# Feed-forward of layer 0: stores of x without waits on each other, issued later, behind the fetch of raw weights; sums for ternary weights two steps ahead

## The chip, the cores and the metric

One NeuronCore of a Trainium2 chip runs the whole program. The metric is the device time of one execution in microseconds; the median of several is given. TensorE (PE) does the matmuls, VectorE (DVE), ScalarE (ACT) and GpSimd (POOL) the elementwise work, and SyncE (SP) issues every DMA.

## What is computed

Two transformer layers over x, 4 x 1024 tokens of width 512 (4096 rows), 16 heads. Layer 0 ends with the feed-forward at issue here, layer 1 uses ternary weights that have to be made from the given float weights:

```python
# layer 0, end
x = x + out @ Wout
h2 = layer_norm(x, ln2_g, ln2_b)
x = x + (gelu(h2 @ W1 + b1) @ W2 + b2)          # W1: 512 x 2048, W2: 2048 x 512

# layer 1: every weight of ada1, ada2, qkv, proj, fc1, fc2
def weight_quant(w):
    s = 1.0 / clip(mean(abs(w)), EPS)            # one mean for the whole matrix
    return clip(round(w * s), -1, 1) / s
def adaln(x, c, g, w, b):
    scale, shift = split(bitlinear(c, w, b))     # the products with ada1 and ada2
    return rmsnorm(x, g) * (1 + scale) + shift
```

## The kernel before, in words

The program is a row of stages; each ends in a barrier of all engines. The change is in `stage_fc0`, which runs from about 1545 to 2315 us of the execution. It computes the feed-forward in 8 blocks of 512 rows (i = 0 to 7), and in each block over 16 chunks of 128 hidden units (f). Together that is 128 steps, u = 16 i + f, and every engine has its own loop over u. All order between engines is by semaphores that are written out by hand.

In a step TensorE does `fc1(u)`, 12 matmuls into `pf` (name `mhi`, `mlo`, `w1h`, `w1l` for the two halves of float32 operands), and `fc2(u - 2)`, 12 matmuls into the four accumulators `pacc`. ScalarE makes `w1h`, the gelu `gf` and its high half `gh`. VectorE makes, in this order, `w1l` for step u + 2, `gl` of step u (after ScalarE's `gh`), at f = 1 of the next block the four additions `xM<-pacc,xM` (the new x of the block; semaphore `s_x2`), at f = 2 to 5 one addition `xb<-xM,bpb` each (`with_bias`: x plus the bias of the next projection, into the single buffer `xb2`, so it waits until the store of the previous one has landed), and last one item of side work, `vector_work(*work[u])`.

The side work turns layer 1's weights into ternary ones while the feed-forward runs. The list `work` has for each matrix, in the order ada1, ada2, qkv, proj, fc1, fc2, one `sum` item per piece of 128 x 1024 numbers, then `mean`, then one `tern` item per piece, and for the two ada matrices an `emb` item. A `sum` reduces a piece to `asum`; TensorE adds the partial sums over the partitions (`tensor_work`, into `pmisc`), one step later than the item; `mean` makes the scale on VectorE out of that product; a `tern` item is three VectorE operations on the piece. The matrices have 4, 4, 6, 2, 8 and 8 pieces, so `work` has 72 items before. `tern` of an ada matrix also has a product on TensorE (`pmisc<-tern,cqT`), which waits for it in the step behind.

SyncE's loop `sync_program` issues in step u: the stores of the finished block (`store_x2`, 4 DMAs `s_x<-xM` of 256 KB) at f = 0, one `store_x2b` (`s_x2b<-xb`, 256 KB) at f = 2 to 5, then `sync_work(*work[u + 1])`, which fetches the raw piece for the next item (`wraw`, 512 KB, two buffers, so it waits until VectorE is through with the piece two before), `sync_store(*work[u - 1])`, the store of a ternary piece (256 KB), and the loads of the next block. SyncE is in order: while it waits for one semaphore, nothing behind is issued.

Of the kernel before, what the change touches and what calls it, by code (L numbers as in the profile page):

```python
# [14 lines left out]
NBLK, TPB = T // BLK, BLK // P  # L15
NT = T // P
# [884 lines left out]
def pieces(n):  # L901
    rows, cols = SHAPE[n]
    wide = CH if cols % CH == 0 else D
    tall = CH // wide
    return [(slice(c * P, (c + tall) * P), slice(n0, n0 + wide), wide)
            for c in range(0, rows // P, tall) for n0 in range(0, cols, wide)]


def stage_mlp0(K):

    nc, a, pe, dve, act, pool, sp = K.nc, K.a, K.pe, K.dve, K.act, K.pool, K.sp
    outer = ExitStack()
    with outer:
        sb = lambda name, shape, dt=F32: outer.enter_context(nc.sbuf_tensor(name, shape, dt))
        w1, w2 = sb("w1", [P, DC, F]), sb("w2", [P, FC, D])
        hf = [sb(f"hf{i}", [P, DC, BLK]) for i in range(2)]
        s_hf, s_w = [K.new_sem() for _ in range(2)], K.new_sem()
        stage_outproj(K, w1, w2, hf, s_hf, s_w)
        stage_fc0(K, w1, w2, hf, s_hf, s_w)


def load_h2(K, hf, s_hf, i):

    K.nc.sync.dma_start(hf[i % 2][:], K.h2_s[:, i * BLK:(i + 1) * BLK].rearrange("(c p) t -> p c t", p=P)).then_inc(*s_hf[i % 2].up(16))
# [201 lines left out]
def stage_fc0(K, w1, w2, hf, s_hf, s_w):  # L1126
    nc, a, pe, dve, act, pool, sp = K.nc, K.a, K.pe, K.dve, K.act, K.pool, K.sp
    LAG = 2
    with Stage(K, "M") as S:
# [10 lines left out]
        gl = [S.sb(f"gl{i}", [P, BLK], F32R) for i in range(3)]  # L1140
        bpb, xb2 = S.sb("bpb", [P, D]), S.sb("xb2", [P, D])
        s_bpb, s_xb, s_xbst = S.sem(), S.sem(), S.sem()
        x_l = S.loads("xM", 4, [P, D])
        tern = S.stores("tern", 2, [P, 2 * D], BF16)
        pf_r = S.ps_ring("pf", 3, [P, BLK])
# [5 lines left out]
        half_rows = [slice(32 * half, 32 * half + B) for half in range(2)]  # L1151
        cqT = S.sb("cqT", [P, DC, B], BF16)
        s_b1, s_cond, s_em, s_emst = S.sem(), S.sem(), S.sem(), S.sem()
        s_f1, s_gf, s_gh, s_gl, s_f2, s_x2, s_xst = (S.sem() for _ in range(7))
        s_asum, s_tot, s_totr, s_tern, s_raw, s_cn, s_cT, s_cq, s_ada, s_emb, s_embr = (S.sem() for _ in range(11))
        work = []
        for i, n in TERN_ORDER:
            work += [("sum", i, n, c, piece) for c, piece in enumerate(pieces(n))]
            work.append(("mean", i, n, 0, None))
            work += [("tern", i, n, c, piece) for c, piece in enumerate(pieces(n))]  # L1160
            if n.startswith("ada"):
                work.append(("emb", i, n, 0, None))
# [11 lines left out]
        def sync_work(kind, i, n, c, piece):  # L1174
            if kind == "emb":
                j = i - 4
                sp.wait_ge(s_emb, 2 * j + 2)
                for half, r in enumerate(half_rows):
                    nc.sync.dma_start(K.emb_s[j + 1][:, half, :], cn2[r, :]).then_inc(*s_emst.up(16))
                if j == 0:  # L1180
                    sp.wait_ge(s_emst, 32)
                    load_ada_bias("L1_cond_b_ada2")
                return
            if kind == "mean":
                return
            rows, cols, wide = piece
            buf, s = raw.take(sp, (kind, n, c), 1, (s_raw, at[kind, n, c] + 1))
            nc.sync.dma_start(buf[:].rearrange("p (c n) -> p c n", n=wide), a[SRC[n]][rows, cols].rearrange("(c p) n -> p c n", p=P)).then_inc(*s.up(16))

        def load_ada_bias(name):  # L1190
            for half, r in enumerate(half_rows):
                nc.sync.dma_start(cn2[r, :], a[name][half * D:(half + 1) * D].partition_broadcast(B)).then_inc(*s_em.up(16))

        def sync_store(kind, i, n, c, piece):
            if kind != "tern" or n.startswith("ada"):
                return
            rows, cols, wide = piece
            k = at["store", n, c]
            buf, s = tern.of(k)
            sp.wait_ge(s_tern, k + 1)  # L1200
            nc.sync.dma_start(K.tern_s[n][rows, cols].rearrange("(c p) n -> p c n", p=P),
                              buf[:].rearrange("p (c n) -> p c n", n=wide)).then_inc(*s.up(16))

        def sync_program():
            nc.sync.dma_start(b1T[:], a["L0_cond_b1_cols"]).then_inc(*s_b1.up(16))
            nc.sync.dma_start(bpb[:], a["L1_cond_b_proj"].partition_broadcast(P)).then_inc(*s_bpb.up(16))
            for r in half_rows:
                nc.sync.dma_start(cn2[r, :], a["cond_1024"]).then_inc(*s_cond.up(16))
            sync_work(*work[0])
            nc.sync.dma_start(b2b[:], a["L0_cond_b2"].partition_broadcast(P)).then_inc(*s_b2.up(16))  # L1210
            for u in range(N_STEP):
                i, f = divmod(u, FC)
                if u == 1:
                    sp.wait_ge(s_cT, 1)
                    load_ada_bias("L1_cond_b_ada1")
                if f == 0 and i > 0:
                    store_x2(i - 1)
                if i > 0 and 0 <= f - 2 < TPB:
                    store_x2b(i - 1, f - 2)
                if u + 1 < len(work):  # L1220
                    sync_work(*work[u + 1])
                if 1 <= u <= len(work):
                    sync_store(*work[u - 1])
                if f == 1 and i + 1 < NBLK:
                    if i >= 1:
                        sp.wait_ge(s_hl, DC * i)
                    load_h2(K, hf, s_hf, i + 1)
                if f == 8:
                    for t in range(TPB):
                        rows = rows_of(i, t)  # L1230
                        x, s = x_l.take(sp, (i, t), 1, (s_xst, 16 * (TPB * i + t + 1)), (s_xb, TPB * i + t + 1))
                        nc.sync.dma_start(x[:], K.x1_s[rows, :]).then_inc(*s.up(16))
            store_x2(NBLK - 1)
            for t in range(TPB):
                store_x2b(NBLK - 1, t)
            sp.wait_ge(s_xst, 16 * NT)
            sp.wait_ge(s_xbst, 16 * NT)
            sp.wait_ge(s_emst, 64)
            tern.done(sp)

        def rows_of(i, t):
            return slice(i * BLK + t * P, i * BLK + (t + 1) * P)

        def store_x2(i):
            for t in range(TPB):
                sp.wait_ge(s_x2, TPB * i + t + 1)
                if TPB * i + t:
                    sp.wait_ge(s_xst, 16 * (TPB * i + t))
                nc.sync.dma_start(K.x2_s[rows_of(i, t), :], x_l.at[i, t][0][:]).then_inc(*s_xst.up(16))

        def store_x2b(i, t):
            sp.wait_ge(s_xb, TPB * i + t + 1)
            nc.sync.dma_start(K.x2b_s[rows_of(i, t), :], xb2[:]).then_inc(*s_xbst.up(16))
# [22 lines left out]
                op.then_inc(*s_f2.up())  # L1276

        def tensor_work(kind, i, n, c, piece):
            if kind == "mean":
                q = [m for _, m in TERN_ORDER].index(n)  # L1280
                pe.wait_ge(s_asum, sum(len(pieces(m)) for _, m in TERN_ORDER[:q + 1]))
                if q >= 2:
                    pe.wait_ge(s_totr, q)
                    pe.wait_ge(s_embr, 4)
                elif q == 1:
                    pe.wait_ge(s_embr, 2)
                else:
                    pe.wait_ge(s_cq, 1)
                nc.tensor.matmul(misc[:, 0:len(pieces(n))], K.ones[:], asum[:, 0:len(pieces(n))], start=True, stop=True).then_inc(*s_tot.up())
            if kind == "tern" and n.startswith("ada"):  # L1290
                k = at["store", n, c]
                pe.wait_ge(s_tern, k + 1)
                pe.wait_ge(s_totr, i - 3)
                for half in range(2):
                    op = nc.tensor.matmul(misc[32 * half:32 * half + B, :], cqT[:, c, :], tern.of(k)[0][:, half * D:(half + 1) * D],
                                          start=c == 0, stop=c == DC - 1)
                op.then_inc(*s_ada.up())
# [75 lines left out]
                nc.scalar.activation(gh[u % 3][:], gf[u % 2][:], ACT.Copy).then_inc(*s_gh.up())  # L1373

        def vector_work(kind, i, n, c, piece):
            q = [m for _, m in TERN_ORDER].index(n)
            if kind == "sum":
                buf = raw.ready(dve, (kind, n, c))
# [59 lines left out]
        def vector_program():  # L1438
# [41 lines left out]
            for t in range(TPB):  # L1480
                with_bias(NBLK - 1, t)

        sync_program()
        tensor_program()
        scalar_program()
# [748 lines left out]
```

## Time and profile before

| what | value |
|---|---|
| median of 3 runs | 3868.43 us (3863.33 to 3868.81) |
| the profiled execution, its own time | 3865.6 us |
| its span in the trace | 3863.7 us |
| mean granted TensorE clock | 0.968 |
| TensorE busy over the whole span | 93% |
| VectorE, ScalarE, GpSimd busy | 69%, 60%, 50% |

The profile gives each instruction's start and length in microseconds from the span's start, and for a wait the instruction that ended it. The profiled execution took 1.9 us more than its span, and 2.8 us less than the median of the runs.

### The profile page before, as it was taken

What the parts mean: (1) busy time and instruction counts of PE and PEld (TensorE: products, weight loads), DVE (VectorE), ACT (ScalarE), POOL (GpSimd) and SP (SyncE); (2) the same over time, 40 slices, a digit from 0 to 9 for tenths busy, and PEclk for the clock granted to TensorE, in tenths of its full rate; (3) what the DMA queues carried; (4) which work ended last, traced back from release to release, by engine and by line L of the source; (5) the groups of instructions that cost most, each with busy time, mean ns of one, the idle gap of its engine ahead of it and who ended that gap; (6) DMA issues with size and microseconds to landing.
All of it is one profiled execution on the core that took longest, in us unless ns stands there. A gap on an engine that the chain in (4) does not pass through costs nothing. (4 is left out here: it accounts for less than half of the span.)

```text
span 3863.7 us, 68702 instructions
## 1 busy us (share of the span) xinstructions
PE 3588.0 (93%) x25924; PEld 2519.3 (65%) x25924; DVE 2666.8 (69%) x4271; ACT 2306.9 (60%) x4011; POOL 1921.6 (50%) x2187
## 2 busy tenths in 40 slices
PE   8997999999999989899999986889999999995999
PEld 7885777767777767777778863446666666652555
DVE  4335888888888866667753327867777777755987
ACT  2225888888888855333333326745555555554988
POOL 1003555555555533444444436646666666663554
PEclk9998999999999999999999998979999999997999
DMA  5546333333323139334431116853334333314221
GB/s 187 186 162 164 64 70 64 70 64 69 62 59 64 40 131 338 104 107 155 148 104 44 50 55 234 313 106 73 64 76 81 66 70 79 74 32 137 83 77 50
DMA packets 284776, 403.16 MB, mean 104 GB/s; under 512 B 89704, under 2 KB 146540, under 8 KB 283930
## 3 DMA queue, kind: packets, MB, share of 16 engines
q1 hardware_dynamic: 284448, 398.78, 37.3%
q8 instruction: 207, 3.39, 0.4%
q14 instruction: 121, 0.99, 0.1%
HBM read 248.95 MB, written 148.93 MB: 103 GB/s over the span
## 5 line engine op out<-in xcount | busy, mean ns | idle before, releaser
L634 POOL TENSOR_SCALAR biastile<-dist,ascale 128x1024 f32<-128x1024 f32 x512 | 574.9, 1123 | 489.4 <-DVE mn L588 476.2
L796 ACT ACTIVATE PT<-st 128x512 f32<-128x512 f32 x1024 | 544.9, 606 | 419.1 <-PE st L730 415.3
L810 DVE TENSOR_REDUCE mn<-s 128x1 f32<-128x1024 f32 x512 | 596.4, 1216 | 273.7 <-PE s L720 273.7
L873 POOL TENSOR_TENSOR two<-PT 128x1024 f32<-128x1024 f32 x256 | 603.5, 2377 | 305.0 <-ACT PT L796 304.9
L588 DVE CUSTOM_DVE_ANT_0 Sn<-sp,biastile 128x1024 f32<-128x1024 f32 x512 | 621.9, 1215 | 78.5 <-PE pt L521 46.7
L559 ACT ACTIVATE Sn<-Sn,mn 128x1024 f32<-128x1024 f32 x512 | 586.9, 1146 | 18.9 <-DVE mn L588 18.8
L521 PEld LDWEIGHTS pt<-ident,Sn 128*128 128x128 f32 x4096 | 454.9, 141 | 177.5 <-issue 150.9
L521 PE MATMUL pt<-ident,Sn 128*128 128x128 f32 x4096 | 546.9, 277 | 22.1 <-DVE og L601 22.1
L549 ACT ACTIVATE PT<-pt 128x512 f32<-128x512 f32 x576 | 337.6, 598 | 136.3 <-PE pt L521 126.3
L730 PE MATMUL st<-QS,KS 98*128 98x512 f32 x1024 | 376.4, 425 | 1.3 <-ACT PT L796 1.2
L720 PE MATMUL s<-KS,QS 96*128 96x512 f32 x1024 | 353.7, 428 | 25.3 <-DMA KS<-s_khi 23.6
L1369 ACT ACTIVATE gf<-pf,b1T 128x512 f32<-128x512 f32 x128 | 88.3, 690 | 480.8 <-PE pf L1263 480.8
L551 DVE COPY PT<-pt 128x512 f32<-128x512 f32 x448 | 309.6, 691 | 87.9 <-PE pt L521 81.3
L489 PE MATMUL sp<-KS,QS 97*128 97x512 f32 x1024 | 304.7, 418 | 23.5 <-DMA KS<-cpad 18.9
L1339 POOL TENSOR_SCALAR w2h<-w 128x512 fp32r<-128x512 f32 x128 | 94.1, 735 | 414.0 <-PE pacc L1275 408.0
L510 PE MATMUL po<-PT,Vp 128*32 128x256 f32 x4096 | 273.7, 384 | 27.5 <-ACT ov L572 27.5
L730 PEld LDWEIGHTS st<-QS,KS 98*128 98x128 f32 x1024 | 192.7, 188 | 146.2 <-ACT PT L796 64.9
L1468 DVE TENSOR_TENSOR gl<-gf,gh 128x512 fp32r<-128x512 f32 x128 | 112.8, 881 | 226.4 <-ACT gh L1373 225.9
L741 PE MATMUL po<-PT,Vp 128*32 128x256 f32 x4096 | 247.3, 382 | 0.0
L720 PEld LDWEIGHTS s<-KS,QS 96*128 96x128 f32 x1024 | 176.9, 193 | 99.3 <-DVE mn L810 52.0
L489 PEld LDWEIGHTS sp<-KS,QS 97*128 97x128 f32 x1024 | 174.2, 191 | 50.3 <-issue 19.3
L1275 PE MATMUL pacc<-w2h,gh 128*128 128x512 f32 x512 | 199.6, 390 | 1.1 <-DVE xM L1475 1.1
(257 smaller groups left out, 6503.2 us busy)
## 6 DMA issues: line engine op xcount, KB each, us to landing
QS<-s_qhi SPq DMA_DIRECT2D x128, 256.0 KB, 5.1
KS<-s_khi SPq DMA_DIRECT2D x128, 256.0 KB, 6.9
KS<-s_klo SPq DMA_DIRECT2D x64, 256.0 KB, 6.2
QS<-s_qlo SPq DMA_DIRECT2D x64, 256.0 KB, 6.8
Vp<-s_v SPq DMA_DIRECT2D x64, 256.0 KB, 7.7
s_o<-og SPq DMA_DIRECT2D x32, 512.0 KB, 4.0
xA<-in_x SPq DMA_DIRECT2D x8, 1024.0 KB, 5.9
s_qhi<-qstage SPq DMA_DIRECT2D x32, 256.0 KB, 2.0
```

The costliest lines, as they stand in the source:

```text
L489: op = nc.tensor.matmul(ps[:, g * BLK:(g + 1) * BLK], qs[0:rows_s, j, t * P:(t + 1) * P], ks[0:rows_s, j, g * BLK:(g + 1) * BLK], start=Tr ...
L521: op = nc.tensor.transpose(ps[:, i, :], sn[:, (g * HALF + i) * P:(g * HALF + i + 1) * P], K.ident[:])
L549: nc.scalar.activation(dst, src, ACT.Copy).then_inc(*s_cp_act.up())
L551: nc.vector.tensor_copy(dst, src).then_inc(*s_cp_dve.up())
L559: nc.scalar.activation(sn[:], sn[:], ACT.Exp, scale=-1.0, bias=mn[n % 3][:, t:t + 1], accum_out=sums[n % 5][:, t:t + 1]).then_inc(*s_exp.up())
L588: nc.vector.tensor_tensor_reduce(sn[:], sp_r.at[s][:], bt[s % 2][:], 1.0, 3.4e38, ALU.add, ALU.min, m).then_inc(*s_min.up())
L634: nc.gpsimd.tensor_scalar(bt[s % 2][:], dist[:, t, :], K.ascale[:, n % H:n % H + 1], 1.0, ALU.mult, ALU.mult).then_inc(*s_bias.up())
L720: op = nc.tensor.matmul(ps[:, g * BLK:(g + 1) * BLK], qs[0:ROWS, j, t * P:(t + 1) * P], ks[0:ROWS, j, g * BLK:(g + 1) * BLK], start=True, ...
L730: nc.tensor.matmul(ps[:], ks_l.at[p][0][0:ROWS + 2, j, kb * P:(kb + 1) * P], qs_l.at[p][0][0:ROWS + 2, j, g * BLK:(g + 1) * BLK], start=Tr ...
L796: nc.scalar.activation(pT[n % 2][:, kb, g * BLK:(g + 1) * BLK], pst_r.at["st", u, g][:], ACT.Exp, scale=-1.0).then_inc(*s_exp.up())
L810: nc.vector.tensor_reduce(mn[n % 2][:, t:t + 1], ps_r.at[u][:], AX.X, ALU.min).then_inc(*s_min.up())
L873: nc.gpsimd.tensor_tensor(two[m % 6][:], pT[n % 2][:, 2 * k, :], pT[n % 2][:, 2 * k + 1, :], ALU.add).then_inc(*s_two.up())
```

## The change

The four stores of a block get a semaphore each, `s_xst[t]`, in place of one for all, and no longer wait for each other's landing. `store_x2` is issued at f = 2 in place of 0 and `store_x2b` at f = 3 to 6 in place of 2 to 5, and both now stand behind `sync_work` and `sync_store` of the step in place of ahead of them. Between the last `sum` and the `mean` of each matrix the list `work` gets two more items, `total` (TensorE's product over the partitions is tied to it) and `rest` (nothing). `work` has 84 items in place of 72, and every item behind the first matrix's sums moves back by 2 steps per matrix.

```diff
+        s_xst = [S.sem() for _ in range(TPB)]
...
-            work.append(("mean", i, n, 0, None))
+            work += [("total", i, n, 0, None), ("rest", i, n, 0, None), ("mean", i, n, 0, None)]
...
-                if f == 0 and i > 0:
-                    store_x2(i - 1)
-                if i > 0 and 0 <= f - 2 < TPB:
-                    store_x2b(i - 1, f - 2)
                 if u + 1 < len(work):
                     sync_work(*work[u + 1])
                 if 1 <= u <= len(work):
                     sync_store(*work[u - 1])
+                if f == 2 and i > 0:
+                    store_x2(i - 1)
+                if i > 0 and 0 <= f - 3 < TPB:
+                    store_x2b(i - 1, f - 3)
...
                 sp.wait_ge(s_x2, TPB * i + t + 1)
-                if TPB * i + t:
-                    sp.wait_ge(s_xst, 16 * (TPB * i + t))
-                nc.sync.dma_start(K.x2_s[rows_of(i, t), :], x_l.at[i, t][0][:]).then_inc(*s_xst.up(16))
+                nc.sync.dma_start(K.x2_s[rows_of(i, t), :], x_l.at[i, t][0][:]).then_inc(*s_xst[t].up(16))
...
         def tensor_work(kind, i, n, c, piece):
-            if kind == "mean":
+            if kind == "total":
```

The places where it meets the path are the changes of block. On SyncE, the one from block 2 to block 3 (steps 48 to 52) reads so before; s34 is `s_x2`, s35 the landing of the previous store, s43 the raw buffer set free, s42 a ternary piece made, s17 `s_xb`:

```order
L1249 DMA s_x<-xM 128x512 [waits s34]
L1249 DMA s_x<-xM 128x512 [waits s35,s34] x3
L1188 DMA wraw<-in_w_fc1T 128x1024 [waits s43]
L1201 DMA s_tfc<-tern 128x1024 [waits s42]
L1188 DMA wraw<-in_w_fc1T 128x1024 [waits s43]
L1201 DMA s_tfc<-tern 128x1024 [waits s42]
L924 DMA hf<-s_h 128x4x512 [waits s9]
L1253 DMA s_x2b<-xb 128x512 [waits s17]
L1188 DMA wraw<-in_w_fc1T 128x1024 [waits s43]
L1201 DMA s_tfc<-tern 128x1024 [waits s42]
```

The four stores stand ahead of the raw fetch, three of them wait for a landing too. After the change SyncE has at the change from block 1 to block 2 (steps 33 to 37), the one that falls into a run of ternary pieces; s46 is the raw buffer, s45 the ternary piece, s38 `s_x2`, s17 `s_xb`:

```order
L924 DMA hf<-s_h 128x4x512 [waits s9]
L1189 DMA wraw<-in_w_qkvT 128x2x512 [waits s46]
L1202 DMA s_tqkv<-tern 128x2x512 [waits s45]
L1249 DMA s_x<-xM 128x512 [waits s38] x4
L1189 DMA wraw<-in_w_qkvT 128x2x512 [waits s46]
L1202 DMA s_tqkv<-tern 128x2x512 [waits s45]
L1253 DMA s_x2b<-xb 128x512 [waits s17]
L1189 DMA wraw<-in_w_qkvT 128x2x512 [waits s46]
L1202 DMA s_tqkv<-tern 128x2x512 [waits s45]
L1253 DMA s_x2b<-xb 128x512 [waits s17]
```

Now the raw fetch goes first, and each `s_x2b` store stands behind a fetch and a ternary store. On VectorE at that same change of block (steps 33 to 35 after the change), s18 is the landing of the previous `s_x2b` store, s38 is `s_x2`:

```order
L1477 TENSOR_TENSOR xM<-pacc,xM 128x512 [waits s37,s15] x4
L1398 TENSOR_SCALAR wraw<-wraw,wsc 128x1024 [waits s6]
L1400 TENSOR_SCALAR wraw<-wraw 128x1024 [waits s2]
L1408 TENSOR_SCALAR tern<-wraw 128x1024 [waits s2]
L1410 ISA [waits s45]
L1334 TENSOR_TENSOR w1l<-w,w1h 128x512 [waits s33,s10]
L1470 TENSOR_TENSOR gl<-gf,gh 128x512 [waits s35]
L1438 TENSOR_TENSOR xb<-xM,bpb 128x512 [waits s18,s38]
L1398 TENSOR_SCALAR wraw<-wraw,wsc 128x1024 [waits s7]
L1400 TENSOR_SCALAR wraw<-wraw 128x1024 [waits s2]
L1408 TENSOR_SCALAR tern<-wraw 128x1024 [waits s2]
L1410 ISA [waits s45]
```

Here a ternary piece follows the four additions and each `xb`; before, this change of block had two `sum` pieces and a `mean` in these steps. The ternary pieces that fall on a change of block are those of ada2 (from step 19), qkv (33 to 37) and fc2 (80 to 83) now, and were those of ada2, fc1 and fc2 before.

## Rows read from the trace of the kernel before

**Rows 1.** The page, busy microseconds of each engine over the span
```profile
PE 3588.0 (93%) x25924; PEld 2519.3 (65%) x25924; DVE 2666.8 (69%) x4271; ACT 2306.9 (60%) x4011; POOL 1921.6 (50%) x2187
```

**Rows 2.** Timeline of TensorE: start, length; first matmuls of `fc1` in some steps
```profile
1651.41 1.20 PE L1263 MATMUL pf<-mhi,w1h 128*128 128x512 f32 x4
...
1657.38 1.20 PE L1263 MATMUL pf<-mhi,w1h 128*128 128x512 f32 x4
...
1679.60 1.20 PE L1263 MATMUL pf<-mhi,w1h 128*128 128x512 f32 x4
...
1756.84 1.07 PE L1263 MATMUL pf<-mhi,w1h 128*128 128x512 f32 x4
...
1787.46 1.07 PE L1263 MATMUL pf<-mhi,w1h 128*128 128x512 f32 x4
...
1858.44 1.07 PE L1263 MATMUL pf<-mhi,w1h 128*128 128x512 f32 x4
...
1868.96 2.07 PE L1263 MATMUL pf<-mhi,w1h 128*128 128x512 f32 x4 [4.92 <-DVE w1l L1334]
...
1877.04 1.07 PE L1263 MATMUL pf<-mhi,w1h 128*128 128x512 f32 x4
...
1882.48 1.07 PE L1263 MATMUL pf<-mhi,w1h 128*128 128x512 f32 x4
...
1953.46 1.07 PE L1263 MATMUL pf<-mhi,w1h 128*128 128x512 f32 x4
...
1972.34 1.07 PE L1263 MATMUL pf<-mhi,w1h 128*128 128x512 f32 x4
```

**Rows 3.** Timeline of VectorE, changes of block 2 to 3 and 4 to 5
```profile
1853.59 2.48 DVE L1475 TENSOR_TENSOR xM<-pacc,xM 128x512 f32<-128x512 f32 x4
1865.66 0.98 DVE L1396 TENSOR_SCALAR wraw<-wraw,wsc 128x1024 f32<-128x1024 f32 x1 [9.60 <-DMA wraw<-in_w_fc1T]
...
1868.21 0.69 DVE L1334 TENSOR_TENSOR w1l<-w,w1h 128x512 fp32r<-128x512 f32 x1
...
2042.60 2.48 DVE L1475 TENSOR_TENSOR xM<-pacc,xM 128x512 f32<-128x512 f32 x4
```

**Rows 4.** Timeline of SyncE's DMA queue, change of block 2 to 3
```profile
1854.30 6.49 SPq L1249 DMA_DIRECT2D s_x<-xM  x4
1860.84 0.42 SPq L1188 DMA_DIRECT2D wraw<-in_w_fc1T  x1
```

**Rows 5.** 10 us: busy PE, PEld, DVE, ACT, POOL; granted clock, DMA share, GB/s
```profile
1860.00:1870.00 10.00, 5.08 (x21) 3.85 (x20) 4.16 (x6) 1.84 (x3) 2.56 (x3) 0.88 0.84 282
```

**Rows 6.** Groups by line, 1540 to 2320: busy us, mean ns; idle before
```profile
L1381 DVE TENSOR_REDUCE asum<-wraw 128x1 f32<-128x1024 f32 x32 | 38.7, 1211 | 19.1 <-DMA wraw<-in_w_projT 9.4 <-DMA wraw<-in_w_ada2T 7.1 <-DMA wraw<-in_w_qkvT 2.0
L1396 DVE TENSOR_SCALAR wraw<-wraw,wsc 128x1024 f32<-128x1024 f32 x32 | 30.4, 951 | 29.4 <-DMA wraw<-in_w_fc1T 10.5 <-DMA wraw<-in_w_fc2T 10.0 <-DMA wraw<-in_w_ada2T 8.9
...
L1398 DVE TENSOR_SCALAR wraw<-wraw 128x1024 f32<-128x1024 f32 x32 | 26.1, 816 | 1.1
...
L1388 DVE TENSOR_REDUCE wmean<-pmisc 128x1 f32<-128x4 f32 (+3 forms) x6 | 1.0, 163 | 32.2 <-PE pmisc L1289 32.2
```

**Rows 7.** The tile `wraw`: duration ns min/median/max, first and last start
```profile
L1396 DVE TENSOR_SCALAR wraw<-wraw,wsc x32: 740/748/1778, 1591.7 to 1990.0; 128x1024 f32<-128x1024 f32 x32
```

**Rows 8.** DMA issues: KB each, median us to landing; 1733:1751, 1861:1863, then 1880:1888
```profile
s_tqkv<-tern SPq DMA_DIRECT2D x4, 256.0 KB, 4.3
...
hf<-s_h SPq DMA_DIRECT2D x1, 1024.0 KB, 8.0
...
s_x2b<-xb SPq DMA_DIRECT2D x2, 256.0 KB, 2.1
s_tfc<-tern SPq DMA_DIRECT2D x2, 256.0 KB, 5.2
```

**Rows 9.** The stage's end: VectorE's second `xb`, and SyncE's last stores
```profile
2306.65 0.69 DVE L1436 TENSOR_TENSOR xb<-xM,bpb 128x512 f32<-128x512 f32 x1 [6.35 <-DMA s_x2b<-xb]
...
2297.69 6.50 SPq L1249 DMA_DIRECT2D s_x<-xM  x4
```

More of the change, by code:

```diff
@@ L1153, in stage_fc0 @@
         s_b1, s_cond, s_em, s_emst = S.sem(), S.sem(), S.sem(), S.sem()
-        s_f1, s_gf, s_gh, s_gl, s_f2, s_x2, s_xst = (S.sem() for _ in range(7))
+        s_f1, s_gf, s_gh, s_gl, s_f2, s_x2 = (S.sem() for _ in range(6))
         s_asum, s_tot, s_totr, s_tern, s_raw, s_cn, s_cT, s_cq, s_ada, s_emb, s_embr = (S.sem() for _ in range(11))
@@ L1183, in sync_work @@
                 return
-            if kind == "mean":
+            if kind in ("total", "rest", "mean"):
                 return
@@ L1230, in sync_program @@
                         rows = rows_of(i, t)
-                        x, s = x_l.take(sp, (i, t), 1, (s_xst, 16 * (TPB * i + t + 1)), (s_xb, TPB * i + t + 1))
+                        x, s = x_l.take(sp, (i, t), 1, (s_xst[t], 16 * (i + 1)), (s_xb, TPB * i + t + 1))
                         nc.sync.dma_start(x[:], K.x1_s[rows, :]).then_inc(*s.up(16))
@@ L1235, in sync_program @@
                 store_x2b(NBLK - 1, t)
-            sp.wait_ge(s_xst, 16 * NT)
+            for sem in s_xst:
+                sp.wait_ge(sem, 16 * NBLK)
             sp.wait_ge(s_xbst, 16 * NT)
@@ L1278, in tensor_work @@
         def tensor_work(kind, i, n, c, piece):
-            if kind == "mean":
+            if kind == "total":
                 q = [m for _, m in TERN_ORDER].index(n)
@@ L1375, in vector_work @@
         def vector_work(kind, i, n, c, piece):
+            if kind in ("total", "rest"):
+                return
             q = [m for _, m in TERN_ORDER].index(n)
```

## The prediction

> **What bounds the kernel now.** I read the page first: TensorE is busy 93% of the span [rows 1], so a change that adds no matmul can win only where TensorE stands or runs slow. The change is confined to one stage, so next comes TensorE's timeline there, one row for the start of `fc1` in each step. The reader is to see the distance between starts: 5.44 us in a step that nothing disturbs (1877.04 to 1882.48 in [rows 2]). At four places it is longer, always about three steps behind a change of block:
>
> - i = 1: steps 18 and 19 take 1679.60 - 1657.38 = 22.2 us. Steps with an ada product run at about 5.97 here (1651.41 to 1657.38), so the loss is 22.2 - 11.9 = 10.3 us.
> - i = 2: steps 34 to 37 take 30.6 us for 4 x 5.44 = 21.8: loss 8.9.
> - i = 3: steps 51 and 52 take 1877.04 - 1858.44 = 18.6 for 10.9: loss 7.7.
> - i = 4: steps 67 and 68 take 18.9 for 10.9: loss 8.0.
>
> The sum is 34.9 us [rows 2]. In i = 3 the wait itself is 4.92 us and ended by `w1l`; the other 2.8 us are matmuls behind it at the lower clock (the four behind the wait take 2.07 in place of 1.07 us, and the 10 us around it show a mean granted clock of 0.88) [rows 2, 5].
>
> The cause is read backwards at i = 3. Step 49 starts two steps before 1858.44, at 1847.56. VectorE finishes its four additions at 1856.1 and then stands 9.60 us for a raw piece [rows 3]. SyncE issued that piece's fetch only at 1860.84, because the four stores ahead of it took from 1854.30 on, three waiting for a landing [rows 4]. So the ternary piece ends late, `w1l` for step 52 starts at 1868.21 and is done at 1868.9, 5.0 us after step 52 was due (1863.9). This gives the rule for the rest: VectorE may end the work of step u, plus 0.7 us of `w1l`, as late as three steps (16.3 us) after TensorE began step u; beyond that TensorE stands.
>
> **The change, part by part.** I count time from TensorE's start of the step with the additions (step 16 i + 1), called 0.
>
> *Stores out of the way of the fetch.* The fetch for step 16 i + 1 is now issued before SyncE waits for the additions, and VectorE finds it landed. This removes the whole chain above at all four places: -34.9 us, if nothing takes its place. Fetches at f = 2 to 5 also no longer wait for `xb`.
>
> *What takes its place.* `store_x2b(t)` now stands behind the fetch of its step, and this waits until VectorE is through with the previous step's item. Its landing sets the single buffer `xb2` free, and `xb` of the next step waits for that, ahead of that step's item. That is a loop: item ends, fetch, (ternary store), `x2b` store lands, `xb`, item. Issued ahead of a fetch the store lands in 2.1 us; stores issued right behind one need 4.3 to 5.2 [rows 8]. The 1 MB load `hf` behind four such DMAs needed 8.0, while 282 GB/s moved [rows 8, 5]. So I take a queue in which what stands ahead is moved first, at 0.28 MB/us, and a landing 1.2 us behind the last byte (2.1 less 0.9 for 256 KB). Behind a fetch alone the store lands 4.8 us after the item's end (0.45 for SyncE's issue and 4.3); behind a fetch and a ternary store another 256 KB is ahead, 5.7. Upper bounds, from the 5.2: 5.7 and 6.6. Lower bound, if loads and stores do not hold each other up: 2.1 and a little. I take 4.8 and 5.7, for the rows lie there.
>
> A ternary piece costs VectorE 0.95 + 0.82 and, for the third operation, of the same shape and taken as the second, 0.82, together 2.6, a sum 1.2, 1.3 with its hand-over [rows 6]; `xb`, `w1l`, `gl` 0.6 to 0.7 each (`xb` is 0.69 long [rows 9]). Undisturbed, the four additions start 5.0 after the step (2042.60; step 81 starts 12 steps behind 1972.34) and take 2.5 [rows 2, 3].
>
> - i = 2, now in a run of ternary pieces: item 33 ends at 7.5 + 2.6 = 10.1, item 34 at 10.1 + 1.9 + 2.6 = 14.6. From 10.1 the queue has a fetch, a ternary store and the four `x2` stores, 1.8 MB, until 16.7, then fetch, store and `x2b`, 3.7 us: landed at 21.6. Item 35 ends at 24.8, item 36 at 24.8 + 5.7 + 0.6 + 2.6 = 33.7, item 37 at 42.6. `w1l` for step 39 is done at 34.4, due at 32.6: 1.8 us; for step 40 at 43.3, due at 38.1 + 1.8: 3.4. With 2.6 of low clock behind it, as measured at i = 3, the loss is 7.8, nearly the 8.9 of now. Bounds: 0, and 10.5 with the slower landings (item 37 at 45.3).
> - i = 1: the ternary pieces stand at steps 19 to 22, without stores, and `xb` for t = 0 falls on the mean. Item 19 ends at 19.1, 20 at 27.1, 21 at 35.1; TensorE wants item 21 for its product at 33.7 (22nd step's start 28.2, one 5.44 step of matmuls). Loss 1.4, which I take without a fall of the clock. Bounds 0, and 3.2 with the slower landings and 2.6 of clock, 5.8.
> - i = 3 and 4 now have sums: items end at 8.8, 12.0, 20.3, 27.0 and at most 33.7, and `w1l` is done 3.7 us before it is due. No loss; the slower landings take 2.7 of the 3.7.
> - i = 5 is a new place with raw pieces, since the list is 12 items longer: 81 ends at 10.1, 82 at 14.6, 83 at about 23, due at 26.5. No loss.
>
> *Sums two steps ahead.* The mean's six waits for TensorE's product, 32.2 us, go [rows 6]. They are VectorE's idle time inside the 16.3 us of room, and the steps around them show no loss beyond the product itself. Gain 0. The moves it makes are counted above. The 12 more items cost nothing: 84 is less than 128.
>
> *End of the stage.* Block 7's four stores took SyncE from 2297.69 to 2304.2, and only then came the first `x2b` store, for which `xb` stood 6.35 us [rows 9]. The fourth addition ends at 2299.7, so this store can now be issued at about 2300.4 and the chain of four that ends the stage begins 3.8 us earlier; with 0.2 us for the fuller queue, -3.6. Bounds: -2.6 (a further 256 KB in the queue) and -3.8. Nothing hides it: the barrier follows.
>
> **Sum.** -34.9 + 7.8 + 1.4 - 3.6 = -29.3. The profiled execution took 3865.6, so 3836.3; it stood 2.8 below the median of the runs, so the median to expect is 3839.
>
> **A page against the trace.** In the Trainium skill, "DMA: Bandwidth & Descriptors", section "Queues, rings and completion order", each DMA engine takes the descriptors of one ring in order; this is the rule that speaks against the change, and the rows on landings agree with it. The same page ("Anatomy of one DMA") fits a DMA's time as 2.0 us plus bytes over 436 GB/s. The trace differs: 282 GB/s in a full stretch. By the page, an estimate, fetch, ternary store and `x2b` together land in 4.4 us in place of 5.7, item 37 would end at 37.1, and i = 2 would lose nothing.
>
> **Rivals.**
> - *No new wait* (22%): the `x2b` store passes the fetch, or the queue is fast enough. For it: alone it lands in 2.1 us. Against: 4.3 to 5.2 behind a fetch. Then -34.9 - 3.6: 3827 by the profile, 3830 for the median.
> - *VectorE itself is too slow at the change of block* (12%). The longest of its ternary operations took 1.78 us, against a median of 0.75 [rows 7]; GpSimd was at work beside it. If pieces 33 to 37 took 5.1 in place of 2.6 us each, i = 2 would lose 12.5 more, and the three at i = 1 7.5 + 2.6 more: gain 6.7, 3862. Against: the mean is 0.95 with such operations in it.
> - *Slower* (5%): the `xb` loop becomes the clock of all changes of block. At i = 3 and 4 it costs TensorE the 8 us that it loses now when each landing takes about 9 us; each further us costs 3 at i = 2, 3, 4 and 2 at i = 1, 11 in all. At 10 us: i = 3 and 4 13 each, i = 2 22, i = 1 14, together 62 against 34.9, less 3.6: +23, 3892. Against: 8.0 us is the longest landing seen here, with 2.5 MB in the queue.
> - *In between* (9%): a second piece of waiting at i = 1 or 5 that I have not seen, gain 8 to 18: 3850 to 3860. That the fetch would still stand behind the stores is excluded by the order of SyncE's rows.
>
> My forecast has the other 52%, 3832 to 3846 (the bounds of i = 1 and i = 2). The range, 3826 to 3853, adds "no new wait" and the near part of "in between". Differences under 0.2% (7.7 us) can hardly be told from none by this measurement; faster than that 0.90, within 0.05, slower 0.05.
>
> **What the new profile would show.** VectorE's waits for `wraw` behind the additions gone; SyncE's waits for landings of `s_x<-xM` gone; `wmean`'s wait near 0; a longer wait of `xb` for `s_x2b<-xb`, its landings at 4 to 6 us in steps 35 to 37; steps 51, 52, 67, 68 at 5.44; a loss of 5 to 10 us around step 40; TensorE's last matmul of the stage 26 us earlier, the barrier 29. I am wrong if the steps behind i = 3 or 4 are still long, or if `w1l` is late at step 40 for another cause than `xb`.

## The result, and the profile after

The changed kernel takes 3837.68 us (median of 4 runs, 3829.55 to 3840.03), the kernel before 3866.47 beside it. The ratio is 0.992, 95% interval 0.9907 to 0.9933. The forecast was 3839. The profiled execution took 3840.03 against 3865.6, 25.6 us less; its span is 3838.0.

TensorE's timeline, the starts of `fc1` at the changes of block from 1 to 2 and 2 to 3, answers to [rows 2] (in all fences: start, length; in brackets the idle time ahead and what ended it). The same source line can stand one or two lines lower than before.

```profile
1771.20 1.07 PE L1263 MATMUL pf<-mhi,w1h 128*128 128x512 f32 x4
...
1778.50 1.19 PE L1263 MATMUL pf<-mhi,w1h 128*128 128x512 f32 x4 [1.70 <-DVE w1l L1334]
...
1789.56 2.08 PE L1263 MATMUL pf<-mhi,w1h 128*128 128x512 f32 x4 [5.32 <-DVE w1l L1334]
...
1796.71 1.07 PE L1263 MATMUL pf<-mhi,w1h 128*128 128x512 f32 x4
...
1862.25 1.07 PE L1263 MATMUL pf<-mhi,w1h 128*128 128x512 f32 x4
...
1867.69 1.07 PE L1263 MATMUL pf<-mhi,w1h 128*128 128x512 f32 x4
...
1873.13 1.07 PE L1263 MATMUL pf<-mhi,w1h 128*128 128x512 f32 x4
```

Behind i = 3 the starts are 5.44 us apart, and so they are behind i = 4: the stalls of step 52 and 68 are gone. Behind i = 2 there is a new pair of waits, 1.70 and 5.32 us at steps 39 and 40. With the slow matmuls behind the second (2.08 in place of 1.07 us) the three steps from 1771.20 take 25.5 us for 16.3: a loss of 9.2, where 8.9 was lost before. The clock granted in the four us from 1789 on was 0.50, its lower level (1.2 GHz); here the columns are the length, the busy time of PE, PEld, DVE, ACT and POOL, the granted clock, the DMA share and GB/s:

```profile
1789.00:1793.00 4.00, 3.44 (x8) 2.78 (x9) 3.82 (x7) 0.00 (x0) 0.00 (x0) 0.50 0.73 224
```

At i = 1 TensorE waits 2.97 us for a ternary piece, the steps 21 to 23 take 21.2 us for 17.9, and 3.3 us are lost:

```profile
1688.34 0.38 PE L1295 MATMUL pmisc<-tern,cqT 128*4 128x512 bf16 x2 [2.97 <-DVE tern L1408]
```

VectorE in those steps answers to [rows 3]; 1744.0 is the start of step 33, five steps ahead of 1771.20:

```profile
1748.98 2.47 DVE L1477 TENSOR_TENSOR xM<-pacc,xM 128x512 f32<-128x512 f32 x4
1751.37 0.87 DVE L1398 TENSOR_SCALAR wraw<-wraw,wsc 128x1024 f32<-128x1024 f32 x1
...
1764.86 0.69 DVE L1438 TENSOR_TENSOR xb<-xM,bpb 128x512 f32<-128x512 f32 x1 [4.29 <-DMA s_x2b<-xb]
1765.47 0.75 DVE L1398 TENSOR_SCALAR wraw<-wraw,wsc 128x1024 f32<-128x1024 f32 x1
1766.25 0.98 DVE L1400 TENSOR_SCALAR wraw<-wraw 128x1024 f32<-128x1024 f32 x1
1767.27 1.66 DVE L1408 TENSOR_SCALAR tern<-wraw 128x1024 bf16<-128x1024 f32 x1
...
1774.62 0.69 DVE L1438 TENSOR_TENSOR xb<-xM,bpb 128x512 f32<-128x512 f32 x1 [4.28 <-DMA s_x2b<-xb]
...
1784.88 0.69 DVE L1438 TENSOR_TENSOR xb<-xM,bpb 128x512 f32<-128x512 f32 x1 [4.74 <-DMA s_x2b<-xb]
1785.49 1.75 DVE L1398 TENSOR_SCALAR wraw<-wraw,wsc 128x1024 f32<-128x1024 f32 x1
```

The ternary piece now follows the additions at once (it stood 9.60 us at i = 3 before), and the waiting has moved to `xb`, three times over 4 us. SyncE's queue shows why; answers to [rows 4]:

```profile
1759.24 0.38 SPq L1189 DMA_DIRECT2D wraw<-in_w_qkvT  x1
1759.67 0.47 SPq L1202 DMA_DIRECT2D s_tqkv<-tern  x1
1760.18 0.47 SPq L1253 DMA_DIRECT2D s_x2b<-xb  x1
...
1769.01 0.37 SPq L1189 DMA_DIRECT2D wraw<-in_w_qkvT  x1
1769.43 0.47 SPq L1202 DMA_DIRECT2D s_tqkv<-tern  x1
1769.94 0.47 SPq L1253 DMA_DIRECT2D s_x2b<-xb  x1
```

Item 34 ends at 1759.15, the store goes out third at 1760.18 and the addition that waits for it starts at 1764.86: 5.7 us from the item's end. Item 35 ends at 1768.93, and the same three go out again: the loop. The stores' landings, in the windows 1769:1772 and 1777:1780 (KB each, median us to landing):

```profile
s_x2b<-xb SPq DMA_DIRECT2D x1, 256.0 KB, 4.6
...
s_x2b<-xb SPq DMA_DIRECT2D x1, 256.0 KB, 6.3
```

against 2.1 ahead of a fetch [rows 8]. The groups by line (1530 to 2320) have the sums of it, and answer to [rows 6]:

```profile
L1383 DVE TENSOR_REDUCE asum<-wraw 128x1 f32<-128x1024 f32 x32 | 38.7, 1210 | 6.4 <-DMA wraw<-in_w_qkvT 3.8 <-DMA wraw<-in_w_ada2T 2.6
L1398 DVE TENSOR_SCALAR wraw<-wraw,wsc 128x1024 f32<-128x1024 f32 x32 | 34.8, 1088 | 0.0
...
L1438 DVE TENSOR_TENSOR xb<-xM,bpb 128x512 f32<-128x512 f32 x32 | 23.1, 722 | 44.0 <-DMA s_x2b<-xb 44.0
```

VectorE's waits for raw pieces went from 19.1 + 29.4 us to 6.4. Its waits for the `x2b` store rose to 44.0, from 23.1 before (same window, kernel before):

```profile
L1436 DVE TENSOR_TENSOR xb<-xM,bpb 128x512 f32<-128x512 f32 x32 | 26.0, 814 | 23.1 <-DMA s_x2b<-xb 23.1
```

The end of the stage, answers to [rows 9]:

```profile
2277.09 0.68 DVE L1438 TENSOR_TENSOR xb<-xM,bpb 128x512 f32<-128x512 f32 x1
2280.01 0.69 DVE L1438 TENSOR_TENSOR xb<-xM,bpb 128x512 f32<-128x512 f32 x1 [2.24 <-DMA s_x2b<-xb]
```

The second `xb` waits 2.24 us in place of 6.35.

For all that follows two numbers are read from each profile: A, from the first to the last of the 128 starts of `fc1`, and B, from there to the next stage's first load of x. They leave out the other stages. Those (the span less A and B) took 3105.7 to 3112.5 us in the twelve profiled executions, 3108.2 and 3111.3 in two executions of the changed kernel itself. A and B come from one profiled execution of each kernel, so the medians stand beside them.

| kernel | A | B | median of the runs | ratio to before (95%) |
|---|---|---|---|---|
| before | 729.0 | 27.5 | 3866 to 3868 | 1 |
| changed | 706.3 | 23.5 | 3837.68 | 0.992 (0.9907 to 0.9933) |
| `changed_again` | 703.4 | 23.5 | 3838.57 | 0.9924 (0.9911 to 0.9936) |
| `waits_only` | 706.7 | 23.5 | 3843.06 | 0.994 (0.9928 to 0.9953) |
| `sums_only` | 721.6 | 27.5 | 3863.28 | 0.999 (0.9981 to 0.9999) |
| `x2_moved` | 697.1 | 23.5 | 3833.24 | 0.9915 (0.9902 to 0.9928) |
| `x2b_first` | 694.1 | 23.5 | 3832.52 | 0.9911 (0.9897 to 0.9925) |
| `two_xb2` | 694.2 | 18.6 | 3823.78 | 0.9888 (0.9875 to 0.9902) |
| `two_xb2_old_sums` | 694.9 | 18.6 | 3824.84 | 0.9891 (0.9878 to 0.9904) |
| `four_xb2` | 693.1 | 17.2 | 3821.86 | 0.9882 (0.987 to 0.9895) |
| `waits_back` | 713.5 | 27.4 | 3853.2 | 0.9967 (0.9955 to 0.998) |
| `waits_back_two_xb2` | 693.2 | 22.7 | 3828.53 | 0.9897 (0.9882 to 0.9913) |

A and B of before are 2287.86 - 1558.88 and 2315.32 - 2287.86 in its timeline. The change took 22.7 from A and 4.0 from B, 26.7 together, and the profiled executions differ by 25.6: the gain lies in this stage.

### The profile page after: what moved, and what is told of

The parts are those of the page before. It is cut to its first block and busy times, and to the rows that moved or that the text cites. A ratio compares the mean times of both kernels' runs of the same rounds, so it can differ in the third digit from the quotient of the medians.

```text
span 3838.0 us, 68678 instructions
## 1 busy us (share of the span) xinstructions
PE 3578.2 (93%) x25924; PEld 2512.9 (65%) x25924; DVE 2660.2 (69%) x4271; ACT 2306.7 (60%) x4011; POOL 1924.8 (50%) x2187
## 5 line engine op out<-in xcount | busy, mean ns | idle before, releaser
L559 ACT ACTIVATE Sn<-Sn,mn 128x1024 f32<-128x1024 f32 x512 | 586.9, 1146 | 19.1 <-DVE mn L588 19.0
L720 PE MATMUL s<-KS,QS 96*128 96x512 f32 x1024 | 353.6, 428 | 25.5 <-DMA KS<-s_khi 23.8
L489 PE MATMUL sp<-KS,QS 97*128 97x512 f32 x1024 | 304.6, 418 | 23.1 <-DMA KS<-cpad 19.0
L510 PE MATMUL po<-PT,Vp 128*32 128x256 f32 x4096 | 273.7, 384 | 27.5 <-ACT ov L572 27.5
L1470 DVE TENSOR_TENSOR gl<-gf,gh 128x512 fp32r<-128x512 f32 x128 | 102.6, 801 | 258.6 <-ACT gh L1373 258.2
L1275 PE MATMUL pacc<-w2h,gl 128*128 128x512 f32 x512 | 199.2, 389 | 0.0
```

The costliest lines, as they stand in the source:

```text
L489: op = nc.tensor.matmul(ps[:, g * BLK:(g + 1) * BLK], qs[0:rows_s, j, t * P:(t + 1) * P], ks[0:rows_s, j, g * BLK:(g + 1) * BLK], start=Tr ...
L559: nc.scalar.activation(sn[:], sn[:], ACT.Exp, scale=-1.0, bias=mn[n % 3][:, t:t + 1], accum_out=sums[n % 5][:, t:t + 1]).then_inc(*s_exp.up())
L720: op = nc.tensor.matmul(ps[:, g * BLK:(g + 1) * BLK], qs[0:ROWS, j, t * P:(t + 1) * P], ks[0:ROWS, j, g * BLK:(g + 1) * BLK], start=True, ...
```

## The experiments

**Is the loss that is left the loop through `xb2`?** `two_xb2` breaks the loop:

```diff
-        bpb, xb2 = S.sb("bpb", [P, D]), S.sb("xb2", [P, D])
+        bpb, xb2 = S.sb("bpb", [P, D]), [S.sb(f"xb2{i}", [P, D]) for i in range(2)]
-        s_bpb, s_xb, s_xbst = S.sem(), S.sem(), S.sem()
+        s_bpb, s_xb, s_xbst = S.sem(), S.sem(), [S.sem() for _ in range(2)]
...
-            if k:
-                dve.wait_ge(s_xbst, 16 * k)
-            nc.vector.tensor_tensor(xb2[:], x_l.at[i, t][0][:], bpb[:], ALU.add).then_inc(*s_xb.up())
+            if k >= 2:
+                dve.wait_ge(s_xbst[k % 2], 16 * (k // 2))
+            nc.vector.tensor_tensor(xb2[k % 2][:], x_l.at[i, t][0][:], bpb[:], ALU.add).then_inc(*s_xb.up())
```

> The changed kernel with two buffers xb2 (a semaphore each) in place of one. Theory: the loss that is left at i = 1 and i = 2 (about 3 and 9 us in the changed kernel's trace) is the loop through the single buffer: the addition xb waits for a store that stands behind a fetch. With two buffers these waits (3.7 to 4.7 us each) go, steps 38 to 40 run at 5.4 us, and the chain at the end of the stage is shorter by about two landings (4 us): 12 + 4 less, profiled about 3822. Rival: VectorE's own load at i = 2 (ternary pieces with operations of 1.7 us beside GpSimd) makes the loss: then steps 38 to 40 still lose 5 us or more and the time is 3830 or above.

A is 694.2, 12.1 less than in the changed kernel, and B 4.9 less; 3823.78 us. In its timeline of VectorE `xb` follows TensorE's steps at 5.45 us, without a wait:

```profile
1754.15 0.68 DVE L1440 TENSOR_TENSOR xb<-xM,bpb 128x512 f32<-128x512 f32 x1
...
1759.61 0.69 DVE L1440 TENSOR_TENSOR xb<-xM,bpb 128x512 f32<-128x512 f32 x1
...
1765.06 0.68 DVE L1440 TENSOR_TENSOR xb<-xM,bpb 128x512 f32<-128x512 f32 x1
```

No step outside the ada products is over 5.6 us. The loop made the whole loss; VectorE's own load made none, although the ternary operations there are longer than before (below). The interval of the ratio, 0.9875 to 0.9902, lies clear of the changed kernel's.

`x2b_first` keeps the one buffer and takes the store out from behind the fetch:

```diff
+                if i > 0 and 0 <= f - 3 < TPB:
+                    store_x2b(i - 1, f - 3)
                 if u + 1 < len(work):
                     sync_work(*work[u + 1])
...
-                if i > 0 and 0 <= f - 3 < TPB:
-                    store_x2b(i - 1, f - 3)
```

> The changed kernel, but the x2b store of a step (f = 3 to 6) is issued ahead of that step's fetch and not behind it; still one buffer xb2. Theory: the store then lands in 2.1 us and xb waits for nothing that matters: the losses of 3 and 9 us at i = 1 and 2 go, about 3827. Rival (VectorE's own load at i = 2): the 9 us stay, 3835 or above.

A is 694.1, the same as with two buffers. The store ahead of the fetch and not behind it is worth 12 us of A (9 against the repeat, `changed_again`). The median, 3832.52, is 5.5 above the 3827 expected, and only 5 to 6 us below those of the changed kernel; the intervals of the two ratios overlap. A and B of the profiled execution are as expected, and its other stages took 4.3 us longer than in the changed kernel's, which is within their spread.

**What did each part of the change do?** `waits_only` is the kernel before without the waits of the stores on each other:

```diff
-                if TPB * i + t:
-                    sp.wait_ge(s_xst, 16 * (TPB * i + t))
-                nc.sync.dma_start(K.x2_s[rows_of(i, t), :], x_l.at[i, t][0][:]).then_inc(*s_xst.up(16))
+                nc.sync.dma_start(K.x2_s[rows_of(i, t), :], x_l.at[i, t][0][:]).then_inc(*s_xst[t].up(16))
```

> The kernel before, with only the waits of the four x2 stores on each other taken away (a semaphore each); places and list as before. Theory A (what counts is how late the fetch is, against the 16.3 us of room): the fetch goes out about 4.2 us earlier (about 0.5 us behind the fourth addition), VectorE's waits for raw pieces fall from 9.6 to about 5.4, TensorE's stall of 4.9 falls to about 0.7 and with it the low clock: 28 of the 34.9 us at the changes of block go, and 3.6 at the end of the stage: about 3834, as much as the whole change. Theory B (it is the position behind the fetch that pays): less than 4.2 us at each of four places, at most 17 and 3.6, 3846 or above.

A is 706.7: by itself this part takes 22.3 us from A, as much as the whole change, and B is 23.5 as there. The four stores of the change to block 3 keep SyncE 2.11 us in place of 6.49, and the fetch behind them goes out 2.9 us after the additions began (1844.90), where it was 7.2 before:

```profile
1845.61 2.11 SPq L1249 DMA_DIRECT2D s_x<-xM  x4
1847.77 0.46 SPq L1189 DMA_DIRECT2D wraw<-in_w_fc1T  x1
```

TensorE's waits behind the four changes of block are

```profile
1669.18 0.38 PE L1295 MATMUL pmisc<-tern,cqT 128*4 128x512 bf16 x2 [4.12 <-DVE tern L1406]
...
1767.50 1.19 PE L1263 MATMUL pf<-mhi,w1h 128*128 128x512 f32 x4 [0.68 <-DVE w1l L1334]
...
1856.20 1.20 PE L1263 MATMUL pf<-mhi,w1h 128*128 128x512 f32 x4 [0.84 <-DVE w1l L1334]
...
1945.72 1.20 PE L1263 MATMUL pf<-mhi,w1h 128*128 128x512 f32 x4 [1.30 <-DVE w1l L1334]
```

At i = 2 to 4 they are 0.68 to 1.30 us in place of 4.7 to 4.9, and the matmuls behind them take 1.2 in place of 2.1 us. A fetch some 4 us earlier is enough, because the room of three steps swallows the rest. Theory B allowed at most 17 us of A and falls by that. The expected 28 us were too much: some 6 were gained at each of i = 2 to 4 and 4.4 at i = 1, where the product has less room and TensorE still waits 4.12 us. The time is less clear than A: the median, 3843.06, is 9 above the 3834 expected and about 5 above the changed kernel's. The other stages took 4.1 us more in its profiled execution than in the changed kernel's, and A and B show no difference.

`sums_only` is the kernel before with the new list alone.

```diff
-            work.append(("mean", i, n, 0, None))
+            work += [("total", i, n, 0, None), ("rest", i, n, 0, None), ("mean", i, n, 0, None)]
...
-            if kind == "mean":
+            if kind == "total":
```

> The kernel before, with only the list changed (total and rest ahead of each mean). Theory: VectorE's six waits for the product (32 us) go and gain nothing by themselves; what changes is which item falls on a change of block: none at i = 1 (loss 0 in place of 10), a ternary piece at i = 2 (about 8.5), sums at i = 3 and 4 (about 6.4 each), and a new place at i = 5 (7.7): 29 in place of 34.9, about 3860. Rival: the waits for the product were on the path, then 20 us or more are gained, 3846 or less.

A is 721.6, so 7.4 us less, and the median, 3863.28, is within 0.2% of before. The six waits of `wmean`, some 32 us, are gone, but the 20 us or more of the rival did not come: the losses at the changes of block are what moved. TensorE's waits are

```profile
1769.71 2.08 PE L1263 MATMUL pf<-mhi,w1h 128*128 128x512 f32 x4 [4.51 <-DVE w1l L1334]
...
1862.90 1.47 PE L1263 MATMUL pf<-mhi,w1h 128*128 128x512 f32 x4 [3.17 <-DVE w1l L1334]
...
1954.76 1.22 PE L1263 MATMUL pf<-mhi,w1h 128*128 128x512 f32 x4 [2.66 <-DVE w1l L1334]
...
2048.50 2.08 PE L1263 MATMUL pf<-mhi,w1h 128*128 128x512 f32 x4 [4.51 <-DVE w1l L1334]
```

4.51 where a ternary piece falls on the change of block, about 3 where a sum does, and a fifth place at i = 5. At i = 1 I had expected nothing, and some 5 us were lost: the first `x2b` store was ready at 1665.3 but went out only at 1669.03, behind the four `x2` stores (1659.73 to 1668.50) and the 1 MB load `hf`, and the next `xb` waited 5.32 us for it. The fault is of the same kind as my forecast's loop, a store for which the single buffer waits, and I had not looked for it there.

`x2_moved` takes the `x2` stores of the change (no waits, behind the fetch) and leaves the `x2b` stores and the list as they were:

```diff
-                if f == 0 and i > 0:
-                    store_x2(i - 1)
                 if i > 0 and 0 <= f - 2 < TPB:
                     store_x2b(i - 1, f - 2)
                 if u + 1 < len(work):
                     sync_work(*work[u + 1])
                 if 1 <= u <= len(work):
                     sync_store(*work[u - 1])
+                if f == 2 and i > 0:
+                    store_x2(i - 1)
```

> Of the change only the x2 stores: no waits on each other, issued at f = 2 behind the fetch; the x2b stores keep their old place (f = 2 to 5, ahead of the fetch) and the list of items is the old one. Theory (late fetches cause the loss, the x2b store behind a fetch causes the new one, the list is worth nothing by itself): neither loss is there; only the 1.1 us remains that TensorE waits for the additions at i = 2, since a ternary piece stands ahead of them. From the first to the last start of fc1 about 695 us (before 729.0, changed 706.3), profiled about 3831. Rival (the sums two ahead free VectorE on the path): at least 5 us more than that, 700 or above.

A is 697.1, 2 us above the forecast and 9 below the changed kernel. TensorE's waits in it are small ones, the largest the additions at i = 2:

```profile
1752.33 0.47 PE L1275 MATMUL pacc<-w2h,gh 128*128 128x512 f32 x1 [1.14 <-DVE xM L1475]
```

So the other half of the change, the `x2b` stores behind the fetch with the new list, gave 9 us of A back (6 against the repeat). The medians, 3833.24 against 3837.68 and 3838.57, point the same way, but the intervals of the ratios overlap. There is no run of the `x2b` stores behind the fetch with one buffer and the old list. By the order of the code it would stand still: at i = 1 SyncE would wait for the `emb` item of step 19, and VectorE in that step for an `x2b` store that stands behind this wait.

`two_xb2_old_sums` is `two_xb2` with the old list:

```diff
-            work += [("total", i, n, 0, None), ("rest", i, n, 0, None), ("mean", i, n, 0, None)]
+            work.append(("mean", i, n, 0, None))
```

> The kernel with two buffers xb2 and with the old list (no total, no rest). Theory: the list decides only which items fall on a change of block, and with two buffers no store is waited for: from first to last start of fc1 about 695.5 us (two buffers with the new list: 694.2), profiled about 3825. Rival: ternary pieces of 5 steps in each of the changes 3 and 4 (they come back there) overload VectorE, or its 30 us of waits for the product reach TensorE: 700 or more, 3830 or more.

A is 694.9 against 694.2: without the loop the list is worth 0.7 us of A, and the medians, 3824.84 and 3823.78, can't be told apart. VectorE's waits for the product are back in it (33.9 us in its list of waits, six times) and cost nothing.

**Do the landings' waits cost anything once they stand behind the fetch?** `waits_back` puts them back into the changed kernel:

```diff
+                if t:
+                    sp.wait_ge(s_xst[t - 1], 16 * (i + 1))
                 nc.sync.dma_start(K.x2_s[rows_of(i, t), :], x_l.at[i, t][0][:]).then_inc(*s_xst[t].up(16))
```

> The changed kernel with the waits of the four x2 stores on each other put back, now behind the fetch. Theory (the waits hurt only by what is queued behind them): at the changes of block the fetch behind is late by about 4 us, inside the 16 us of room, so 706 us from first to last start of fc1 as in the changed kernel, and 3.6 us more at the end of the stage: profiled about 3842. Rival (the waits hurt wherever they stand): 10 us or more on top, 3850.

A is 713.5, 7.2 us more than in the changed kernel, and not the same: the expectation was wrong in A, right in B (27.4, 3.9 more). The median is 3853.2 (3846.97 to 3860.45), nearer to the rival's 3850 than to 3842. TensorE loses about 3 us more than in the changed kernel at i = 1, as much at i = 4, and 1 at i = 3 and 5 together. I had followed the fetch behind the waits, which has room, and not the `x2b` store, which has none. At i = 3 SyncE's queue and VectorE show it:

```profile
1864.20 0.42 SPq L1189 DMA_DIRECT2D wraw<-in_w_fc1T  x1
1864.68 0.44 SPq L1255 DMA_DIRECT2D s_x2b<-xb  x1
...
1869.26 1.27 DVE L1440 TENSOR_TENSOR xb<-xM,bpb 128x512 f32<-128x512 f32 x1 [7.34 <-DMA s_x2b<-xb]
```

The store goes out at 1864.68, 7.6 us after its addition's end (1857.1), and `xb` waits 7.34. If that is the way, a second buffer must take all of it away; that is `waits_back_two_xb2`, the two diffs of `two_xb2` and `waits_back` together.

> The kernel with the waits of the x2 stores put back behind the fetch, and with two buffers xb2. Theory (those waits cost 7 us at the changes of block only because they hold up the x2b store, for which the single buffer waits): with two buffers the cost is gone: 694 to 696 us from first to last start of fc1, as with two buffers without the waits (694.2), and at the end of the stage 3.9 us more than there. Rival: the later fetch behind the stores costs by itself, then 700 us or more.

A is 693.2: the 7 us are gone, and the rival falls. B is 22.7, 4.0 more than without the waits.

`four_xb2` has four buffers:

```diff
-        bpb, xb2 = S.sb("bpb", [P, D]), S.sb("xb2", [P, D])
-        s_bpb, s_xb, s_xbst = S.sem(), S.sem(), S.sem()
+        bpb, xb2 = S.sb("bpb", [P, D]), [S.sb(f"xb2{i}", [P, D]) for i in range(4)]
+        s_bpb, s_xb, s_xbst = S.sem(), S.sem(), [S.sem() for _ in range(4)]
```

> The changed kernel with four buffers xb2. At the changes of block nothing more than with two (694.2 us). At the end of the stage the four additions xb follow each other and their stores go out together: the next stage's first load starts about 16.5 us after the last start of fc1 in place of 18.6, profiled 2 us less than with two buffers, about 3822.

A is 693.1 and B 17.2, 1.5 below two buffers where 2.1 was expected. 3821.86 us is the fastest of all, 0.9882 of before, though it and `two_xb2` can't be told apart by their medians. `changed_again` is the repeat:

> The changed kernel once more, beside the others on one chip: 706.3 us from first to last start of fc1, 23.5 from there to the next stage's first load, median 3838 within 3 us. If the loss at i = 1 and 2 were chance, 706.3 would move by several us.

A is 703.4 and B 23.5, the median 3838.57. TensorE waits in the same steps: 2.97 us for the product at i = 1, the same to 0.01 us; at i = 2 one wait of 3.16 us in place of 1.70 and 5.32, a loss of 6.4 in place of 9.2. The loss is no chance, but its size at i = 2 varies by 3 us.

## Why the prediction was right

The forecast rested on four terms, and each was found where it was put; two of them were larger.

- *The 34.9 us of late fetches.* All four stalls went. Six kernels in which no late fetch and no loop reaches TensorE (`x2_moved`, `x2b_first` and the four with more than one buffer) have A between 693.1 and 697.1, 32 to 36 us less than before.
- *The loop behind the fetch at i = 2*, forecast 7.8, was 9.2 and 6.4. By its parts, counted from the step with the additions: item 35 ended at 24.9 (forecast 24.8), item 36 at 33.4 (33.7), item 37 at 44.7 (42.6); TensorE waited 1.70 and 5.32 (1.8 and 3.4). That items 35 and 36 came out so close is partly luck. In the round of item 36 it took 5.7 us from an item's end to `xb`, as forecast. In the round of item 35 it also took 5.7, where the forecast had 7.0 for the four `x2` stores in the queue. Against that, item 34 ended 0.5 us late and the work of item 35 took 4.1 us and not 3.2, with operations of 0.98 and 1.66 us. In the last round it took 7.45, because the store landed in 6.3 us, and then an operation took 1.75; why the same three DMAs landed their store in 4.6 us one time and in 6.3 the next, no run shows. The low clock cost 1.7 more, not 2.6.
- *The product at i = 1*, forecast 1.4, was 3.3. Term mis-sized: the loop without a ternary store took 5.0 and 5.2 us from an item's end to `xb` (4.8), and items 19 and 21 each had two operations at 1.0 and 1.6 to 1.7 us, so that item 19 ended 1 us and item 21 two us later than forecast.
- *No loss at i = 3, 4, 5*: none. *The end of the stage*, -3.6: -4.0.
- *Sums two steps ahead, worth 0 by themselves*: `two_xb2_old_sums` shows it, 0.7 us of A apart. What the list did is to put sums on i = 3 and 4, and ternary pieces on i = 2.

Together A and B fell by 26.7 for 29.3: the losses at i = 1 and 2 had been put 1.9 and 1.4 too low, and the gain at the end 0.4 too low. That the median came out 1.3 us from the forecast is luck in part: the profiled execution, 3840.03, is 3.7 above its forecast of 3836.3. I had added 2.8 us from there to the median, as before, but this execution was the slowest of its four runs, 2.35 above the median.

The rival "no new wait" is the kernel with two buffers, and `two_xb2` reached less than its 3830 because the buffer also shortened B. The rival in VectorE's own load, with ternary operations at 1.78 us, is half real: they became longer, and it cost nothing as long as no store was waited for. In the rival "slower" one step does not follow from the others: 8 us at a landing of 9 and 3 for each further one give 11 at i = 3 and 4, not 13. It did not enter the forecast.

The prediction also sets its queue against the fit in the Trainium skill, "DMA: Bandwidth & Descriptors", section "Anatomy of one DMA". That section gives the fit for DMAs issued by GpSimd, which the prediction leaves out; here SyncE issues them. The estimate of 4.4 us for fetch, ternary store and `x2b` store was too short in this trace: from the issue of the fetch (1759.24) to the `xb` that waits for the landing (1764.86) it took 5.6. The 0.28 MB/us put in its place is a mean, and no fixed rate: the 10 us from 1754 on moved 284 GB/s, the two us from 1758 on 406.

The first half of the change was the gain and the second a cost: `x2_moved`, less than half of the diff, is 6 to 9 us better in A than the whole, and 4 to 5 in the median, which alone would not tell them apart.

## What to carry to other kernels

When a DMA is moved behind another on an in-order queue, ask for both what waits for its landing: here the fetch had 16 us of room and the store none, because it freed the only buffer of the next step. A late transfer costs only what goes beyond the room of its consumer, so a cheap cut that brings it nearly inside the room (dropping three waits) took as much from this stage as the whole change. One more buffer of 256 KB in the loop was worth as much at the changes of block as the better order of the queue (A 694.2 and 694.1), and 4.9 us more at the end of the stage.

## What the runs showed that was not expected

VectorE's ternary operations are not of one length. The same instruction on the same shape takes from 0.69 to 1.7 us, and how often it is long depends on where it falls: with the old list the second of the three operations averaged 0.82 us before and 0.85 in `x2_moved`, with the new list 1.03 in the changed kernel and 1.10 in `two_xb2`:

```profile
L1402 DVE TENSOR_SCALAR wraw<-wraw 128x1024 f32<-128x1024 f32 x32 | 35.1, 1097 | 1.1
```

GpSimd works on `w2` in every step, and the trace of the changed kernel ties the two together. Of the 96 ternary operations there, the 27 long ones (1.4 us or more) had a GpSimd operation beside them for 1.4 us on average, the 20 of 0.8 to 1.4 us for 0.9, and every one of these 47 had some; the 49 short ones had it for 0.05 us, and 36 of them not at all. That the two hold each other up is likely; no run took GpSimd's work away, so it is not shown.

TensorE's clock did not fall with every wait, and the length of the wait alone does not decide it. Behind the waits of 0.68 to 1.70 us the first four matmuls took 1.2 us and the granted clock stayed at 1.00 (2.4 GHz), and so it did behind the 2.97 us at i = 1 in the changed kernel. Behind 4.51, 4.92 and 5.32 us they took 2.1, and the clock was 0.50 (1.2 GHz) at once. Between these it went both ways. In `changed_again` a wait of 3.16 was followed by a full 2.1:

```profile
1780.01 2.08 PE L1263 MATMUL pf<-mhi,w1h 128*128 128x512 f32 x4 [3.16 <-DVE w1l L1334]
```

In `sums_only` the first four matmuls behind 2.66 us took only 1.22, but the next eight ran at the lower level:

```profile
1955.81 1.88 PE L1263 MATMUL pf<-mlo,w1h 128*128 128x512 f32 x4
1957.49 1.90 PE L1263 MATMUL pf<-mhi,w1l 128*128 128x512 f32 x4
```

```profile
1956.00:1958.00 2.00, 2.00 (x6) 1.52 (x6) 1.89 (x3) 0.00 (x0) 0.00 (x0) 0.50 1.06 389
```

So a wait of 2.66 us was followed by a fall and one of 2.97 was not; what decides it stays open.
